# Layer 2's scan: six odd states with a drive scaled by ScalarE and turned by TensorE, y and raw steps in two bank pairs by turns

## The chip, the cores and the metric

The kernel runs on one core of one Trainium2 chip. The metric is the device time of the whole program in microseconds. Engines are named as in the profile: PE is TensorE, PEld its weight loads, DVE is VectorE, ACT is ScalarE, POOL is GpSimd, SP is SyncE. All data here is float32.

## The reference, cut to what matters

x has 16 samples of 64 x 64 places and 128 channels. Four layers are added to it one after the other: linear attention, a Fourier mixing, a selective scan in four directions (layer 2, the one that is changed), and a gated scan in one direction. Layer 2 in short:

```python
xs = stack([x0, x1, x0[..., ::-1], x1[..., ::-1]], axis=1)   # 4 directions, 256 channels, 4096 places
x_dbl = einsum('bkdl,kcd->bkcl', xs, x_proj_w)
dts_r, Bs, Cs = x_dbl[:, :, :R], x_dbl[:, :, R:R + N], x_dbl[:, :, R + N:]   # R = 8, N = 16
dt = softplus(einsum('bkrl,kdr->bkdl', dts_r, dt_proj_w) + dt_proj_b)
def step(h, inp):
    dA = exp(dt_l[..., None] * A)
    h = h * dA + (dt_l * u_l)[..., None] * B_l[:, :, None, :]
    y = einsum('bkdn,bkn->bkd', h, C_l)
    return (h, y)
ys = ys + Ds * xs
```

## The kernel before, in words

A hardware loop runs once per sample; each sample goes through the four layers. The scan of layer 2 (class Scan2, and a function scan2 on each engine) works in **groups**: one group g is one direction k and one chunk c of 512 places, 4 x 8 = 32 groups a sample. Its 256 channels are two halves h of 128 partitions, side by side in 1024 columns. A **unit** u is one of the 16 states n of a group, so there are 512 units a sample. For every unit:

- POOL makes the drive (make_drive, L545): du times the row of B, spread over the partitions by a DMA, into one of six SBUF buffers Q. In front of it stand sum_dt (L528) and make_du (L535) once a group.
- ACT makes the decays (L1026 through act): exp(A dt) of both halves into one of two bank pairs of PSUM, banks 2, 3 or 4, 5 by turns.
- DVE runs two scans (states, L1568). For the states in POOL_STATES the result goes to Q and POOL weighs it with the row of C (weigh, L556); for the others it stays in PSUM and DVE weighs it (weigh, L1576) into Q.
- ACT copies the last column of the state (carry) for the next chunk.
- PE adds Q onto y with an identity matrix (L662), into banks 0 and 1.

Once a group, for the next group, PE multiplies rows of dt, B and C (rows, bank 6), ACT copies them (split), PE makes the raw steps (steps, banks 7 and 6), ACT and DVE work out softplus in two halves: ACT gives abs, exp, relu, the mask, a square and a log (three parts each of two activations, 512 columns), and log_small on DVE (L1533, L1536) puts a series where the log is inexact. DVE takes y out of PSUM in take_y (L1545 in direction 0, L1553 in the others).

The order of the work is written out by hand: every engine has its own list over u, and semaphores tie them. The decays of unit u + 2 wait until unit u has left the same bank pair, a drive waits until the sum of the unit six before has been made, and each engine works its list strictly in order. SP issues the loads of B and C rows, two rows to a DMA, in rings of four buffers each.

Of the kernel before, what the change touches and what calls it, by code (L numbers as in the profile page):

```python
# [20 lines left out]
KDIR = 4  # L21
# [5 lines left out]
POOL_STATES = (1, 4, 6, 9, 12, 14)  # L27
# [40 lines left out]
def program(nc, x_in, consts, d, out):  # L68
# [6 lines left out]
    with ctx:  # L75
# [27 lines left out]
        DTB2 = sb("DTB2", KDIR * 2); AN2 = sb("AN2", KDIR * 2 * SN)  # L103
# [137 lines left out]
        class Scan2:  # L241
# [8 lines left out]
            def __init__(s):  # L250
# [16 lines left out]
                s.b_loaded = [sample_sem(f"s2_b_loaded{i}") for i in range(4)]  # L267
                s.c_loaded = [sample_sem(f"s2_c_loaded{i}") for i in range(4)]
# [12 lines left out]
                s.y_taken = sample_sem("s2_y_taken")  # L281

# [33 lines left out]
            def wide(s, bufs, u):  # L316

                return bufs[u // 2 % 4][:, NT * (u % 2):NT * (u % 2 + 1)]

            def loads(s, u):  # L320

                return 16 * (u // 8 + 1)
# [12 lines left out]
            def like(s, ap, g):  # L335

                if g // NCH % 2 == 0:
# [69 lines left out]
                 (DTW2[32:32 + RANK, :], d["dtw2"]), (DTB2[:, :], d["dtb2"]), (AN2[:, :], d["al2"]),  # L407
# [1377 lines left out]
```

## Time and profile before

| | us |
|---|---|
| median of 3 runs | 40399.08 |
| lowest and highest | 40380.85, 40405.81 |
| profiled execution, its own time | 40396.46 |
| its span, first to last instruction | 40394.6 |
| granted PE clock, mean over the span | 0.875 |

The profile's page gives the busy time of each engine over the span, then 40 slices, the DMA queues, and groups of instructions by line. Nearly every activation has the same line, since a helper records it, so operands and shapes tell them apart. Sixteen samples give sixteen like stretches; layer 2's scan is the largest part of each. PSUM is PS, the six Q, DT, DU and the softplus buffers are all parts of WORK, XN holds rows of B, CWIDE and WORK hold rows of C, and HST the carried states.

### The profile page before, as it was taken

The page shows a single profiled execution, that of the slowest core. Times are in us where ns is not written, and L with a number is a line of the kernel's source. Part 1 is how long each engine was busy: PE and PEld are TensorE (multiplying, and loading weights), DVE is VectorE, ACT ScalarE, POOL GpSimd, SP SyncE. Part 2 cuts the span into 40 slices and gives each one's busy share as a digit, 9 for nine tenths or more (in the row PEclk, how much of TensorE's full clock was granted, in tenths as well). Part 3 has the DMA queues.
Part 4 walks back from the last instruction along what each step waited for, and adds up shares of the span by engine and source line. Part 5 has one row for each costly group of instructions (what it writes and reads, how often), then busy time and mean ns, then how long its engine had stood idle before and what let it go on. Part 6 is the DMA issues. An engine that isn't in the chain of part 4 may idle for free. (4 is left out here: it accounts for less than half of the span.)

```text
span 40394.6 us, 270531 instructions
## 1 busy us (share of the span) xinstructions
PE 29251.1 (72%) x61476; PEld 11541.5 (29%) x61476; DVE 33936.9 (84%) x33869; ACT 19958.1 (49%) x37509; POOL 30996.0 (77%) x14776
## 2 busy tenths in 40 slices
PE   6777777777777777777777777777777777777777
PEld 3232232322323223232232322323223232232322
DVE  7969879698796987969879698796987969879698
ACT  4545545455454554545545455454554545545455
POOL 6949869498694986949869498694986949769497
PEclk8888888888888888888888888888888888888888
DMA  3424324243242432424324243242432424324243
GB/s 104 151 83 152 135 100 151 85 151 134 100 152 84 152 134 101 152 84 152 134 102 151 83 152 134 101 152 84 151 133 103 151 84 151 133 102 152 84 152 132
DMA packets 1387317, 5029.10 MB, mean 124 GB/s; under 512 B 164272, under 2 KB 165816, under 8 KB 1381440
## 3 DMA queue, kind: packets, MB, share of 16 engines
q1 hardware_dynamic: 1385536, 5010.20, 35.5%
q8 instruction: 526, 8.62, 0.1%
q14 instruction: 1255, 10.28, 0.1%
HBM read 4938.25 MB, written 71.30 MB: 124 GB/s over the span
## 5 line engine op out<-in xcount | busy, mean ns | idle before, releaser
L662 PE MATMUL PS<-WORK,CST 128*128 128x512 f32 x36096 | 19792.8, 693 | 8395.9 <-POOL WORK L556 7606.2
L545 POOL TENSOR_TENSOR WORK<-WORK,XN 128x1024 f32<-128x1024 f32 x8192 | 19253.1, 2383 | 1.3
L662 PEld LDWEIGHTS PS<-WORK,CST 128*128 128x128 f32 x36096 | 7532.0, 220 | 20965.6 <-POOL WORK L556 10427.4
L1026 ACT ACTIVATE PS<-WORK,AN 128x512 f32<-128x512 f32 x17408 | 11307.0, 679 | 1984.9 <-DVE WORK L1576 1092.8
L1568 DVE TENSOR_TENSOR_SCAN PS<-PS,HST,WORK 128x512 f32<-128x512 f32 x8960 | 10975.2, 1272 | 45.4 <-ACT PS L1026 32.1
L1568 DVE TENSOR_TENSOR_SCAN WORK<-PS,HST,WORK 128x512 f32<-128x512 f32 x5376 | 6582.9, 1267 | 0.0
L556 POOL TENSOR_TENSOR WORK<-WORK,CWIDE 128x1024 f32<-128x1024 f32 x2048 | 4864.0, 2375 | 118.3 <-issue 65.2
L1026 ACT ACTIVATE HST<-PS 128x2 f32<-128x2 f32 x5152 | 858.6, 167 | 6586.2 <-DVE WORK L1576 6152.6
L632 POOL MEMSET XN<- 128x66 f32 x32 | 4.9, 154 | 5101.7 <-DVE SM L1414 5003.0
L1576 DVE TENSOR_TENSOR WORK<-PS,WORK 128x1024 f32<-128x1024 f32 x3072 | 3763.0, 1225 | 105.2
L1026 ACT ACTIVATE WORK<-PS 40x512 f32<-40x512 f32 (+2 forms) x1600 | 935.5, 598 | 3547.7 <-PE PS L662 2867.3
L1026 ACT ACTIVATE WORK<-PS,DTB 128x512 f32<-128x512 f32 x2304 | 1556.3, 675 | 2144.3 <-DVE WORK L1536 1650.0
L1576 DVE TENSOR_TENSOR WORK<-PS,CWIDE 128x1024 f32<-128x1024 f32 x2048 | 2508.8, 1225 | 70.0
L556 POOL TENSOR_TENSOR WORK<-WORK 128x1024 f32<-128x1024 f32 x1024 | 2438.1, 2381 | 0.0
L528 POOL TENSOR_TENSOR WORK<-WORK 128x512 f32<-128x512 f32 x1024 | 1326.5, 1295 | 1407.2 <-DVE WORK L1536 1407.2
L662 PE MATMUL PS<-XN,TAP 128*128 128x512 f32 x4608 | 2055.2, 602 | 34.6 <-DVE XN L1430 34.6
L662 PE MATMUL PS<-BIG,XP 128*40 128x512 f32 x2304 | 1687.6, 819 | 451.8 <-ACT BIG L1026 294.5
L601 POOL TENSOR_TENSOR WORK<-WORK 128x512 f32<-128x512 f32 x1024 | 1275.1, 1269 | 840.9 <-DMA WORK<-xbc_rows 774.7
L1026 ACT ACTIVATE WORK<-WORK,VEC 128x512 f32<-128x512 f32 x2304 | 1631.4, 708 | 0.0
L1568 DVE TENSOR_TENSOR_SCAN PS<-PS,WORK 128x512 f32<-128x512 f32 x1280 | 1491.0, 1211 | 109.3 <-POOL WORK L545 104.7
L1026 ACT ACTIVATE WORK<-PS,VEC 128x512 f32<-128x512 f32 x896 | 614.1, 685 | 1693.5 <-PE PS L662 1691.1
L535 POOL TENSOR_TENSOR WORK<-WORK,BIG 128x1024 f32<-128x1024 f32 x512 | 1347.8, 2632 | 1.2
(158 smaller groups left out, 25260.5 us busy)
## 6 DMA issues: line engine op xcount, KB each, us to landing
XN<-xbc_rows SPq DMA_DIRECT2D x4096, 512.0 KB, 3.6
WORK<-xbc_rows SPq DMA_DIRECT2D x2816, 512.0 KB, 4.3
CWIDE<-xbc_rows SPq DMA_DIRECT2D x2304, 512.0 KB, 4.2
BIG<-in_spec_dram SPq DMA_DIRECT2D x32, 2048.0 KB, 12.3
X<-in_x_dram SPq DMA_DIRECT2D x68, 512.0 KB, 4.8
xbc_rows<-WORK SPq DMA_DIRECT2D x512, 64.0 KB, 3.1
out_dram<-X SPq DMA_DIRECT2D x64, 512.0 KB, 5.1
xbc_rows<-WORK SPq DMA_DIRECT2D x128, 32.0 KB, 1.6
```

The source lines that it names most:

```text
L528: nc.gpsimd.tensor_tensor(dt, dt, S.LE[:, ch(h)], ADD).then_inc(S.dt_made, 1)
L535: nc.gpsimd.tensor_tensor(S.like(S.DU[g % 2], g), S.like(S.DT[g % 2], g), S.cols(BIG1, g), MUL).then_inc(S.du_ready, 1)
L545: nc.gpsimd.tensor_tensor(S.both(S.Q[u % 6]), S.both(S.DU[u // SN % 2]), S.wide(S.BW, u).unsqueeze(1).to_broadcast([P, 2, NT]), MUL).then_ ...
L556: nc.gpsimd.tensor_tensor(q, q, S.wide(S.CW, u).unsqueeze(1).to_broadcast([P, 2, NT]), MUL).then_inc(S.weighed_pool, 1)
L601: nc.gpsimd.tensor_tensor(S.Q[u % 6], S.DU[u // SN3 % 2], S.wide(S.BW, u), MUL).then_inc(S.drive, 1)
L632: nc.gpsimd.memset(XN3[:, 0, :], 0.0).then_inc(frame_zero, 1)
L662: return nc.tensor.matmul(o, w, r, start=start, stop=stop)
L1026: return nc.scalar.activation(o, i, f, **k)
L1568: r = V.tensor_tensor_scan(o, a, b, HST2[:, 2 * n + h:2 * n + h + 1] if c else 0.0, MUL, ADD)
L1576: V.tensor_tensor(S.both(S.Q[u % 6]), PS[:, lo:lo + 2, :], S.wide(S.CW, u).unsqueeze(1).to_broadcast([P, 2, NT]), MUL).then_inc(S.weighed_ ...
```

## The change

Six odd states (5, 7, 9, 11, 13, 15) get their drive by another road. After du is made, PE turns it (turn_du, at unit 15 of the group before) so that places lie on partitions, and ACT copies it to SBUF as DUT (copy_dut, at unit 1). The row of B is turned too (turn_b at unit 5, copied by copy_bt at unit 6), so that B's value is one number per partition. For a turned unit ACT scales DUT by it, four activations of 256 columns into one buffer ST (scale), and PE turns the eight blocks back into the unit's bank pair (turn_back). The decays of such a unit go to its Q in SBUF, and the scan reads its drive from PSUM. POOL makes no drive for these states, but weighs nine states where it weighed six. DVE weighs seven where it weighed ten.

y and the raw steps share two bank pairs, 0 and 1 or 6 and 7, by turns of the group. The softplus is done once over 1024 columns in six parts, at units 7 to 11, and its bias comes in through a row of ones in the step matmul. The sum on PE comes two units later than its unit, take_y after unit 2 in place of unit 1, the small log once after unit 11 in place of twice after 7 and 10, and sum_dt once at unit 12. The loads of B and C are one row each, in rings of six.

```diff
-POOL_STATES = (1, 4, 6, 9, 12, 14)
+POOL_STATES = (0, 4, 5, 7, 8, 9, 11, 13, 15)
+TURNED_STATES = (5, 7, 9, 11, 13, 15)
...
+                s.CW = [take(NT) for _ in range(4)] + [CWIDE[:, NT * i:NT * (i + 1)] for i in range(2)]
+                s.ST = CWIDE[:, w:2 * w]
+                s.BW = [XN[:, NT * i:NT * (i + 1)] for i in range(6)]
+                s.DUT = XN[:, 6 * NT:6 * NT + w]
...
+            def pair(s, g):
+                return 0 if g % 2 == 0 else 6
...
+            def wait_pair(s, e, u):
+                if s.on_pool(u):
+                    e.wait_ge(s.scanned, u + 1)
+                else:
+                    s.wait_weighed(e, u)
+                    if s.of(u)[1] < NCH - 1:
+                        e.wait_ge(s.carried, s.carried_by(u))
...
+                def turn_b(g):
+                    e.wait_ge(S.rows_copied, g + 1)
+                    for j in range(4):
+                        r = nc.tensor.transpose(bank(S.pair(g) + 1)[:, SN * j:SN * (j + 1)], S.R[0:SN, ch(j, P)], EYE[0:SN, 0:SN])
+                    r.then_inc(S.b_turned, 1)
...
+                    if h == 1:
+                        e.wait_ge(S.bt_copied, g + 1)
...
+                def turn_back(u):
+                    e.wait_ge(S.scaled, 4 * S.turned_by(u))
+                    if u >= 2:
+                        S.wait_pair(e, u - 2)
+                    for h in range(2):
+                        for j in range(4):
+                            r = nc.tensor.transpose(bank(S.banks(u)[h])[:, ch(j, P)], S.ST[:, ch(2 * j + h, P)], EYE)
+                    r.then_inc(S.turned_back, 1)
...
                 for u in range(S.units):
                     g, n = u // SN, u % SN
                     if g + 1 < KDIR * NCH:
+                        if n == 3:
+                            rows(g + 1, 0)
+                            rows(g + 1, 1)
+                        if n == 5:
+                            turn_b(g + 1)
+                        if n == 6:
+                            steps(g + 1, 0)
+                            steps(g + 1, 1)
+                        if n == 15:
+                            turn_du(g + 1)
+                    if u + 2 < S.units and S.is_turned(u + 2):
+                        turn_back(u + 2)
+                    if u >= 2:
+                        sum_up(u - 2)
...
+                def scale(u):
+                    if u % SN == S.turned[0]:
+                        e.wait_ge(S.dut_copied, u // SN + 1)
+                        e.wait_ge(S.bt_copied, u // SN + 1)
+                    if S.turned_by(u) > 1:
+                        e.wait_ge(S.turned_back, S.turned_by(u) - 1)
+                    for j in range(4):
+                        col = SN * j + u % SN
+                        act(S.ST[:, ch(j, 2 * P)], S.DUT[:, ch(j, 2 * P)], ACT.Identity,
+                            scale=S.BT[u // SN % 2][:, col:col + 1]).then_inc(S.scaled, 1)
...
                 for u in range(S.units):
                     g, n = u // SN, u % SN
-                    if u + 1 < S.units:
-                        decays(u + 1)
+                    if u + 3 < S.units and S.is_turned(u + 3):
+                        scale(u + 3)
+                        decays(u + 3)
+                    if n == 1 and g:
+                        copy_dut(g)
                     if g + 1 < KDIR * NCH:
-                        if n == 2:
+                        if n == 5:
                             split(g + 1)
-                        if 4 <= n < 10:
-                            softplus(g + 1, (n - 4) // 3, (n - 4) % 3)
+                        if n == 6:
+                            copy_bt(g + 1)
+                        if n in (7, 8, 9):
+                            softplus(g + 1, n - 7)
+                        if n == 9:
+                            softplus(g + 1, 3)
+                        if n in (10, 11):
+                            softplus(g + 1, n - 6)
                     if S.of(u)[1] < NCH - 1:
                         carry(u)
+                    if u + 2 < S.units and not S.is_turned(u + 2):
+                        decays(u + 2)
...
+                        a, b = (in_sbuf, in_psum) if S.is_turned(u) else (in_psum, in_sbuf)
+                        o = in_sbuf if S.on_pool(u) else in_psum
```

The first place is ACT, the first group of a sample, units 7 to 10 before: the second half's softplus parts among decays (PS<-WORK,AN) and carries (HST).

```order
L1026 ACTIVATE WORK<-PS,DTB 128x512 [waits s2_dt_steps,s2_dt_raw]
L1026 ACTIVATE WORK<-WORK 128x512 [waits s2_softplus]
L1026 ACTIVATE HST<-PS 128x2 [waits s2_weighed_dve]
L1026 ACTIVATE PS<-WORK,AN 128x512 [waits s2_carried,s2_weighed_dve]
L1026 ACTIVATE PS<-WORK,AN 128x512
L1026 ACTIVATE WORK<-PS,DTB 128x512
L1026 ACTIVATE WORK<-WORK,VEC 128x512 [waits s2_softplus]
L1026 ACTIVATE HST<-PS 128x2 [waits s2_weighed_dve]
L1026 ACTIVATE PS<-WORK,AN 128x512 [waits s2_carried,s2_weighed_dve]
L1026 ACTIVATE PS<-WORK,AN 128x512
```

The same engine after, units 8 to 10: CWIDE<-XN,BTR are scalings, WORK<-WORK,AN the decays of a turned unit, 128x1024 the softplus parts.

```order
L1132 ACTIVATE PS<-WORK,AN 128x512 [waits s2_scanned]
L1132 ACTIVATE PS<-WORK,AN 128x512
L1132 ACTIVATE WORK<-PS 128x1024
L1132 ACTIVATE WORK<-WORK,VEC 128x1024 [waits s2_softplus]
L1132 ACTIVATE HST<-WORK 128x2 [waits s2_scanned]
L1132 ACTIVATE CWIDE<-XN,BTR 128x256 [waits s2_turned_back]
L1132 ACTIVATE CWIDE<-XN,BTR 128x256 x3
L1132 ACTIVATE WORK<-WORK,AN 128x512 [waits s2_summed]
L1132 ACTIVATE WORK<-WORK,AN 128x512
L1132 ACTIVATE PS<-WORK,VEC 128x1024 [waits s2_softplus]
L1132 ACTIVATE HST<-PS 128x2 [waits s2_weighed_dve]
L1132 ACTIVATE PS<-WORK,AN 128x512 [waits s2_carried,s2_weighed_dve]
```

Before, one or two activations of 512 columns stand between two pairs of decays. After, four scalings that wait for turned_back, the decays of a turned unit and up to two parts of 1024 columns stand between the decays of one even unit and the next.

The second place is PE. Before, in the second group, units 2 to 4: sums (WORK,CST), and the step matmuls (WORK,DTW), each behind rows_copied.

```order
L662 MATMUL PS<-WORK,CST 128x512 [waits s2_weighed_dve]
L662 MATMUL PS<-WORK,CST 128x512
L662 MATMUL PS<-WORK,DTW 128x512 [waits s2_rows_copied]
L662 MATMUL PS<-WORK,CST 128x512 [waits s2_weighed_dve]
L662 MATMUL PS<-WORK,CST 128x512
L662 MATMUL PS<-WORK,DTW 128x512 [waits s2_rows_copied]
L662 MATMUL PS<-WORK,CST 128x512 [waits s2_weighed_pool]
L662 MATMUL PS<-WORK,CST 128x512
```

After, in the second group, units 4 to 6: turn_b (CST,ROW), turn_back (CST,CWIDE), the steps (ROW,DTW) and the sums.

```order
L722 MATMUL PS<-WORK,CST 128x512 [waits s2_weighed_dve]
L722 MATMUL PS<-WORK,CST 128x512
L892 MATMUL PS<-CST,ROW 128x16 [waits s2_rows_copied]
L892 MATMUL PS<-CST,ROW 128x16 x3
L919 MATMUL PS<-CST,CWIDE 128x128 [waits s2_scanned,s2_scaled]
L919 MATMUL PS<-CST,CWIDE 128x128 x7
L722 MATMUL PS<-WORK,CST 128x512 [waits s2_weighed_dve]
L722 MATMUL PS<-WORK,CST 128x512
L722 MATMUL PS<-ROW,DTW 128x512
L722 MATMUL PS<-ROW,DTW 128x512 [waits s2_bt_copied]
L722 MATMUL PS<-WORK,CST 128x512 [waits s2_weighed_pool]
L722 MATMUL PS<-WORK,CST 128x512
```

The turn back of unit 7 stands behind turn_b, which waits for ACT's copy of the rows, and the one of unit 9 behind the second step matmul, which waits for bt_copied, and behind a sum.

## Rows read from the trace of the kernel before

**Rows 1.** Page, part 1: busy us (share of the span) and instructions of each engine.

```profile
PE 29251.1 (72%) x61476; PEld 11541.5 (29%) x61476; DVE 33936.9 (84%) x33869; ACT 19958.1 (49%) x37509; POOL 30996.0 (77%) x14776
```

**Rows 2.** Windows: one group; stretch, length, PE, PEld, DVE, ACT, POOL busy (count), PEclk, DMA, GB/s.

```profile
494.70:550.20 55.50, 37.21 (x71) 13.82 (x70) 54.15 (x51) 30.71 (x62) 55.50 (x26) 0.88 0.46 154
```

**Rows 3.** Timeline of POOL: start us, us, engine, line, op, out<-in, count [idle before].

```profile
494.70 1.27 POOL L528 TENSOR_TENSOR WORK<-WORK 128x512 f32<-128x512 f32 x1
...
550.20 1.29 POOL L528 TENSOR_TENSOR WORK<-WORK 128x512 f32<-128x512 f32 x1
...
954.17 2.87 POOL L535 TENSOR_TENSOR WORK<-WORK,BIG 128x1024 f32<-128x1024 f32 x1
...
1010.60 2.87 POOL L535 TENSOR_TENSOR WORK<-WORK,BIG 128x1024 f32<-128x1024 f32 x1
```

**Rows 4.** Timeline of DVE, same columns: scans, weighing, take_y, small log.

```profile
512.20 1.23 DVE L1576 TENSOR_TENSOR WORK<-PS,CWIDE 128x1024 f32<-128x1024 f32 x1
513.34 2.45 DVE L1568 TENSOR_TENSOR_SCAN WORK<-PS,HST,WORK 128x512 f32<-128x512 f32 x2
515.71 2.44 DVE L1568 TENSOR_TENSOR_SCAN PS<-PS,HST,WORK 128x512 f32<-128x512 f32 x2
518.18 1.23 DVE L1576 TENSOR_TENSOR WORK<-PS,CWIDE 128x1024 f32<-128x1024 f32 x1
...
526.34 1.41 DVE L1545 SCALAR_TENSOR_TENSOR BIG<-BIG,VEC,PS 128x512 f32<-128x512 f32 x2 [0.93 <-PE PS L662]
...
546.90 0.69 DVE L1533 SCALAR_TENSOR_TENSOR PS<-PS,WORK 128x512 f32<-128x512 f32 x1
547.63 0.73 DVE L1536 COPY_PREDICATED WORK<-WORK,PS 128x512 f32<-128x512 uint32 x1
...
972.35 2.37 DVE L1553 TENSOR_TENSOR BIG<-BIG,PS 128x1024 f32<-128x1024 f32 x1 [0.88 <-PE PS L662]
```

**Rows 5.** Timeline of ACT, same columns: decays, softplus parts, a carry.

```profile
494.48 1.30 ACT L1026 ACTIVATE PS<-WORK,AN 128x512 f32<-128x512 f32 x2
495.71 0.67 ACT L1026 ACTIVATE WORK<-PS,DTB 128x512 f32<-128x512 f32 x1
496.29 0.71 ACT L1026 ACTIVATE WORK<-WORK,VEC 128x512 f32<-128x512 f32 x1
496.90 0.15 ACT L1026 ACTIVATE HST<-PS 128x2 f32<-128x2 f32 x1
497.14 1.30 ACT L1026 ACTIVATE PS<-WORK,AN 128x512 f32<-128x512 f32 x2
```

**Rows 6.** Groups by form, ACT: shapes xcount, busy us, mean ns, idle before.

```profile
L1026 ACT ACTIVATE BIG<-PS 128x512 f32<-128x512 f32 x768 | 433.2, 597 | 490.4 <-PE PS L662 489.8
...
L1026 ACT ACTIVATE BIG<-PS 128x256 f32<-128x256 f32 x64 | 24.6, 384 | 293.4 <-DVE BIG L1488 293.4
...
L1026 ACT ACTIVATE WORK<-WORK 128x1024 f32<-128x1024 f32 x64 | 62.1, 1043 | 0.0
```

**Rows 7.** Timeline of PE: eight transposes; then records of sums in the scan.

```profile
94.20 1.04 PE L725 MATMUL PS<-CST,WORK 128*128 128x128 f32 x8
...
541.09 3.70 PE L662 MATMUL PS<-WORK,CST 128*128 128x512 f32 x8 [1.53 <-POOL WORK L556]
...
548.00 3.78 PE L662 MATMUL PS<-WORK,CST 128*128 128x512 f32 x4 [3.21 <-POOL WORK L556]
```

**Rows 8.** Windows, columns as in Rows 2: transposes alone, and a start after idle.

```profile
94.00:96.00 2.00, 1.66 (x16) 1.42 (x14) 0.36 (x2) 1.09 (x2) 0.00 (x0) 1.00 0.00 0
...
547.00:550.20 3.20, 2.20 (x3) 1.16 (x4) 3.16 (x5) 1.63 (x4) 3.20 (x2) 0.50 0.71 273
```

More of the change, by code:

```diff
@@ L314, in both, with is_turned, turned_by, decay_of @@
                 return ap.rearrange("p (d l) -> p d l", l=NT)
[L316 to L322, printed above, removed]
+            def is_turned(s, u):
+                return u % SN in s.turned
+            def turned_by(s, u):
+                return u // SN * len(s.turned) + sum(n <= u % SN for n in s.turned)
+            def decay_of(s, u):
+                return s.decay_sbuf if s.is_turned(u) else s.decay
+            def decayed_by(s, u):
+                return s.turned_by(u) if s.is_turned(u) else s.driven_by(u)
+            def driven_by(s, u):
+                return u + 1 - s.turned_by(u)
+            def pair(s, g):
+                return 0 if g % 2 == 0 else 6
+            def raw(s, g):
+                return PS[:, s.pair(g):s.pair(g) + 2, :]
+            def loaded(s, i):
+                return 16 * (i // 6 + 1)
+            def wait_pair(s, e, u):
[5 more added lines that the diff above has]
+                        e.wait_ge(s.carried, s.carried_by(u))
             def position(s, g):
@@ L840, in scan2 @@
                     if g + 1 < KDIR * NCH:
-                        if n < 2:
-                            rows(g + 1, n)
-                        if n in (3, 4):
-                            steps(g + 1, n - 3)
-                    S.wait_weighed(e, u)
-                    if n == 0 and g:
-                        e.wait_ge(S.y_taken, g)
-                    for h in range(2):
-                        r = mm(bank(h), EYE, S.Q[u % 6][:, ch(h)], n == 0, n == SN - 1)
-                    r.then_inc(S.summed, 1)
+                        if n == 3:
[12 more added lines that the diff above has]
+                        sum_up(u - 2)
+                sum_up(S.units - 2)
+                sum_up(S.units - 1)
             def block2():
@@ L1157, in softplus @@
                     elif part == 1:
+                        e.wait_ge(S.softplus, 6 * g + 1)
+                        act(S.E, S.LE, ACT.Exp, scale=-1.0).then_inc(S.softplus, 1)
+                    elif part == 2:
                         if g >= 2:
-                            e.wait_ge(S.decay, 2 * SN * (g - 1))
+                            last = SN * (g - 1) - 1
+                            e.wait_ge(S.decay, 2 * S.driven_by(last))
+                            e.wait_ge(S.decay_sbuf, 2 * S.turned_by(last))
@@ L1557, in states @@
                     k, c, n = S.of(u)
-                    e.wait_ge(S.drive, u + 1)
+                    if S.is_turned(u):
+                        e.wait_ge(S.turned_back, S.turned_by(u))
+                    else:
+                        e.wait_ge(S.drive, S.driven_by(u))
                     if c:
```

243 lines of the change are left out of this document (139 added, 104 removed).

## Prediction

> **What bounds the kernel now.** The page first [rows 1]: VectorE 84% and GpSimd 77% of the span, ScalarE 49%, and the same pattern sixteen times. These shares are averages over four layers. The change touches layer 2's scan alone, so I read one chunk group there (16 units, one chunk of one direction). In the window of one group of direction 0 [rows 2] GpSimd is busy 55.50 of 55.50 us and VectorE 54.15. The timeline of GpSimd [rows 3] gives the period: 494.70 to 550.20 is 55.50 us in direction 0, 954.17 to 1010.60 is 56.43 us in direction 1, where the multiply that makes du reads columns turned (2.87 us). Directions 2 and 3 I take as 0 and 1. GpSimd bounds the stage with VectorE 1.3 us behind. In those 55.50 us stand 16 drives, 6 weighings, one du, each 1024 columns, and two 512-column sums (1.27 us): 23 large operations (the count of 26 takes one in at the edge) at (55.50 - 2 x 1.23) / 23 = 2.31 us.
>
> **Removed from GpSimd.** After: 10 drives, 9 weighings, one sum of 1024 and one du, 21 x 2.31 = 48.5 us (49.1 in odd directions). Seven microseconds go from the engine that bounds.
>
> **VectorE.** Start to start [rows 4]: two scans of a unit that GpSimd weighs take 2.37 us (513.34 to 515.71), the others 2.47 (515.71 to 518.18) and their weighing 1.14 (512.20 to 513.34), 3.61 together. Before 10 x 3.61 + 6 x 2.37 = 50.3; after 7 x 3.61 + 9 x 2.37 = 46.6. The two small-log passes of 0.69 + 0.73 become one of 1024 columns; a VectorE operation of 1024 columns in PSUM takes 1.23 [rows 4], so I take 2.45. take_y stays: 1.4 us (direction 0) or 2.37 (direction 1). No scan has had its decay in SBUF and drive in PSUM; both operand places occur singly, and I price it the same, with +0.06 per scan (1 us a group) as the bad end. VectorE's own work is then 50.4 or 51.4 us. If nothing else were late, that would be the period.
>
> **What is late next is ScalarE.** Two decays of 512 cost 1.23 us (494.48 to 495.71), one activation of 512 0.58 to 0.61, a carry from PSUM with the next decay behind it 0.24 [rows 5]. A column costs (0.597 - 0.384) / 256 = 0.83 ns and 1024 columns 1.04 us in all [rows 6]. So a scaling of 256 columns starts 0.61 - 0.21 = 0.40 after the one before: 1.6 us for the four of a turned unit, 9.6 a group; a softplus part of 1024 takes 1.03, six of them 6.2 instead of 12 x 0.6. ScalarE's sum, near 40 us, fits in 50. Its order does not. I lay the instructions out by these durations, with t = 0 where VectorE starts unit 3 of a group and everything earlier ready.
>
> Eight transposes took 1.04 us [rows 7]; four matmul records of a sum at full clock (x8 in 3.70) 1.7 us. 3.7: unit 3 weighed. Only then ScalarE carries it (the carry stands ahead of the scaling for unit 7), and only then can TensorE turn unit 5 back, into unit 3's banks: 5.0. ScalarE scales 7, makes decays 7, carries 4, makes decays 6: 9.4 (0.25 of it waiting for a sum). split, carry 5: 10.05. TensorE has turn_b **ahead** of turn_back(7), and turn_b waits for split: unit 7 is back at 11.6, and the scaling for 9 waits for that. Scale 9, decays 9, the copy of b, carry 6, decays 8: 16.3. Softplus part 0, carry 7: 17.4. turn_back(9) stands behind the second step matmul, which waits for the copy of b (14.85), and behind sum_up(4): 14.85 + 0.86 + 1.7 + 1.04 = 18.5. Then scale 11, decays 11, part 1, carry, decays 10: 23.8. Parts 2 and 3: 25.9. Scale 13, decays 13, part 4, carry, decays 12: 31.3. Part 5: 32.4. From 3.7 that is 28.7 us, 24.4 of work and 4.3 of waits on TensorE's queue.
>
> VectorE without waits reaches the small log after units 3 to 11, (3, 6 and 10 of 3.61, six of 2.37): 25.0. By the steps above it waits 0.55 before unit 6, 0.9 before 8, 0.35 before 9, 2.4 before 10 and 3.15 before the small log, 7.4 in all. The small log needs part 5, so it ends at 34.85. Units 12 to 15 and 0 to 2 follow at VectorE's pace (4 x 3.61 + 3 x 2.37 = 21.55; ScalarE's four jobs per pair of units are 4.3 us with no softplus among them), take_y 1.35 or 2.3: 57.7 us in direction 0, 58.7 in 1. Waits queued elsewhere are covered: GpSimd's sum of dt waits for the small log, then needs 3 x 2.31 us to the first drive of the next group while VectorE has 12 us of units 12 to 15. SyncE issues 26 loads of one row for 16 of two, less traffic than the 154 GB/s of [rows 2], into rings of six, with weighings six units back to wait for.
>
> **Sum.** +2.2 and +2.3 us a group against 55.50 and 56.43. Of 32 groups a sample the last has no softplus of a next one and gains VectorE's 50.3 - 46.6 = 3.7, say 4 us. 16 x (31 x 2.25 - 4) = 1,050 us. The pieces ahead of the first group and the constants are costed at nothing: the turn of du there hides behind the first drive. The profiled execution took 40,396 us, 3 us under the median shown, so **41,450**.
>
> **Rivals.**
>
> *The chain without its waits.* TensorE's queue costs less than I laid out and only the 24.4 us of work and one turn (1.3) stay. Then part 5 ends at 29.3, and the period is 54.6 or 55.6: -0.85 a group, 39,910 us. For it: each wait is under 2 us and depends on how exactly the engines meet. Against it: the order of TensorE's queue is fixed and turn_b truly waits for split.
>
> *VectorE bounds (faster).* If ScalarE runs ahead more than I allow, so that part 5 is there when unit 11 ends, the period is VectorE's 50.4 or 51.4: -5.1 x 31 - 4 a sample, 37,800 us. It decides when ScalarE needs under 21.3 us for what I count as 24.4 + 1.3. For it: both old bounds shrink for certain. Against it: 17% fewer microseconds than the rows give.
>
> *A slow TensorE (slower still).* The granted clock fell in this stage: after an idle of 1.53 us the eight records took 3.70, after 3.21 us four took 3.78 [rows 7] at a granted 0.50, the 1.2 GHz level [rows 8]. In the new order TensorE sits idle about 7 us before unit 15 is turned, and about 2.8 us twice before unit 5. If units 5 to 11 meet the low clock, the three turns on the chain double (+0.87 each), the step matmul too (+0.86) and sum_up(4) (+1.7): +5.2 a group, 44,000 us. Against it: from 3.7 to 30 TensorE has work two thirds of the time. A stretch of nothing but transposes ran at a granted 1.00 [rows 8], though behind other matmuls. The Trainium skill, TensorE: Matmul & The Clock Gate, Part 4, says that transposes do not count as TensorE activity as matmuls do; by it the 64 new ones would help less to hold the clock, which leans to this rival; the stretch just named neither bears it out nor refutes it.
>
> *No difference.* The layout's gain and the chain's loss cancel within 0.2%, some 80 us, about what a measurement of this kernel can tell from no change.
>
> **Chances.** Forecast 0.53; slow TensorE 0.12; chain without waits 0.16 (0.11 faster, 0.03 same, 0.02 slower); VectorE bounds 0.16; cancelling 0.03. So faster 0.27, same 0.06, slower 0.67. The range takes the forecast, the chain without waits (39,910) and half of the slow TensorE (+2.6 a group, 42,700): 39,850 to 42,700 leaves out VectorE's bound and full slowness, 2 in 10.
>
> **What would show it.** In the profile after: a period near 58 us from du to du; GpSimd no longer full (some 49 busy); ScalarE without gaps over 1.6 us from unit 4 to the small log; VectorE waiting for ScalarE before units 8 and 10 and some 3 us before the small log. Wrong if VectorE has no wait over 1 us before the small log (second rival), if the scalings start over 0.45 or under 0.35 us apart, if eight transposes take about 1.9 us between units 5 and 11 (slow TensorE), or if the waits stand before other units than 6 to 11.

## The result, and the profile after

| | before | after |
|---|---|---|
| median, us | 40402.26 | 42912.14 |
| lowest and highest | 40380.85, 40405.81 | 42883.87, 42947.69 |
| ratio, 95% interval | | 1.0623, 1.0604 to 1.0641 |
| span of the profiled execution | 40394.6 | 42881.9 |

The change makes the kernel 6.2% slower, 2,510 us. The forecast was slower, and 41,450 us; the time lies 212 us above the range. First the page of after, part 1, beside [rows 1], then part 4, the chain that ended last:

```profile
PE 31957.7 (75%) x92196; PEld 14932.2 (35%) x92196; DVE 32162.6 (75%) x30798; ACT 24681.1 (58%) x47749; POOL 27597.9 (64%) x12728
...
PE 34%; ACT 26%; DVE 16%; POOL 11%; issue 10%; DMA 2%; SPq 1%; POOLq 0%; ACTq 0%; DVEq 0%
```

GpSimd and VectorE both lost work, as the change meant, and neither is near full. PE and ACT carry 60% of the chain, which is that of the whole program: the time goes back and forth between the two engines that got the new road of the drive.

Windows of after, columns as in [rows 2]: one group of direction 0 and one of direction 1, each from one multiply that makes du to the next; then three stretches within the first group.

```profile
703.91:765.29 61.38, 45.43 (x132) 21.57 (x132) 50.61 (x45) 39.85 (x81) 48.88 (x21) 0.89 0.35 113
947.44:1009.02 61.58, 45.86 (x132) 20.66 (x132) 51.24 (x44) 39.77 (x81) 49.50 (x22) 0.89 0.35 113
...
735.00:739.50 4.50, 4.01 (x15) 1.85 (x14) 4.42 (x4) 3.50 (x9) 4.50 (x3) 1.00 0.49 131
739.90:746.50 6.60, 6.60 (x14) 3.45 (x14) 2.92 (x3) 2.19 (x6) 2.04 (x1) 0.50 0.38 122
747.00:752.00 5.00, 5.00 (x19) 2.54 (x17) 2.29 (x3) 4.63 (x9) 3.51 (x2) 1.00 0.33 80
```

The period is 61.4 us where 57.7 was forecast; GpSimd is busy 48.9 (48.5 forecast), VectorE 50.6 (50.4), ScalarE 39.9 ("near 40"). So the work of these three engines was priced rightly and the waits were not. The granted clock is 1.00, then 0.50, the 1.2 GHz level, then 1.00 again, in the middle of a stretch in which TensorE is busy.

Timeline of PE in that group, columns as in [rows 3], L919 turn_back, L892 turn_b, the L722 records with ROW the step matmuls, those with WORK,CST the sums:

```profile
728.38 1.09 PE L919 MATMUL PS<-CST,CWIDE 128*128 128x128 f32 x8
729.31 3.60 PE L722 MATMUL PS<-WORK,CST 128*128 128x512 f32 x8
734.42 0.41 PE L892 MATMUL PS<-CST,ROW 16*128 16x16 f32 x4 [1.51 <-ACT ROW L1132]
734.76 1.09 PE L919 MATMUL PS<-CST,CWIDE 128*128 128x128 f32 x8
735.69 1.88 PE L722 MATMUL PS<-WORK,CST 128*128 128x512 f32 x4
737.51 1.12 PE L722 MATMUL PS<-ROW,DTW 9*128 9x512 f32 x2
739.11 1.47 PE L722 MATMUL PS<-ROW,DTW 9*128 9x512 f32 x2 [0.48 <-ACT BTR L1132]
740.51 3.78 PE L722 MATMUL PS<-WORK,CST 128*128 128x512 f32 x4
744.08 1.92 PE L919 MATMUL PS<-CST,CWIDE 128*128 128x128 f32 x8
```

Turning 5 and 7 back runs at full speed (1.09 us). Then the second step matmul takes 1.47, the sum of unit 4 3.78 where its neighbour took 1.88, and turn_back(9) 1.92. ScalarE, same view, at the scalings (CWIDE<-XN,BTR, four records each) of units 7, 9 and 11, and then VectorE at its waits:

```profile
729.51 1.70 ACT L1132 ACTIVATE CWIDE<-XN,BTR 128x256 f32<-128x256 f32 x4 [1.41 <-PE PS L919]
...
735.89 1.71 ACT L1132 ACTIVATE CWIDE<-XN,BTR 128x256 f32<-128x256 f32 x4 [1.44 <-PE PS L919]
...
746.04 1.71 ACT L1132 ACTIVATE CWIDE<-XN,BTR 128x256 f32<-128x256 f32 x4 [4.30 <-PE PS L919]
```

```profile
733.37 2.47 DVE L1717 TENSOR_TENSOR_SCAN PS<-PS,HST,WORK 128x512 f32<-128x512 f32 x2 [0.76 <-ACT PS L1132]
...
740.03 2.46 DVE L1717 TENSOR_TENSOR_SCAN WORK<-PS,HST,WORK 128x512 f32<-128x512 f32 x2 [0.58 <-ACT PS L1132]
746.04 2.45 DVE L1717 TENSOR_TENSOR_SCAN WORK<-WORK,HST,PS 128x512 f32<-128x512 f32 x2 [3.54 <-PE PS L919]
751.20 2.47 DVE L1717 TENSOR_TENSOR_SCAN PS<-PS,HST,WORK 128x512 f32<-128x512 f32 x2 [2.71 <-ACT PS L1132]
...
760.17 1.23 DVE L1678 SCALAR_TENSOR_TENSOR PS<-PS,WORK 128x1024 f32<-128x1024 f32 x1 [2.89 <-ACT WORK L1132]
```

Unit 3 starts on VectorE at 724.18, so these are 5.3, 11.7 and 21.9 us in the forecast's count, which had 5.0, 11.6 and 18.5. Up to turn_back(7) the layout is right within 0.3 us; turn_back(9) is 3.4 late, and everything behind it with it.

### The profile page after: what moved, and what is told of

The parts are those of the page before. It is cut to its first block, busy times and chain, and to the rows that moved or that the text cites. A ratio compares the mean times of both kernels' runs of the same rounds, so it can differ in the third digit from the quotient of the medians.

```text
span 42881.9 us, 337204 instructions
## 1 busy us (share of the span) xinstructions
PE 31957.7 (75%) x92196; PEld 14932.2 (35%) x92196; DVE 32162.6 (75%) x30798; ACT 24681.1 (58%) x47749; POOL 27597.9 (64%) x12728
## 4 chain that ended last, share of the span: by engine, by line
PE 34%; ACT 26%; DVE 16%; POOL 11%; issue 10%; DMA 2%; SPq 1%; POOLq 0%; ACTq 0%; DVEq 0%
PE PS L722 27%; ACT WORK L1132 11%; ACT CWIDE L1132 7%; POOL WORK L608 7%; PE PS L919 6%; ACT PS L1132 6%; POOL WORK L619 4%; DVE PS L1717 4%; DVE WORK L1717 3%; DVE PS L1678 1%; DMA CWIDE<-xbc_rows 1%; DVE PS L1810 1%; ACT BIG L1132 1%; ACT ROW L1132 1%; PE PS L892 0%
## 5 line engine op out<-in xcount | busy, mean ns | idle before, releaser
L722 PE MATMUL PS<-WORK,CST 128*128 128x512 f32 x36096 | 18666.1, 654 | 2490.9 <-POOL WORK L619 2419.0
L608 POOL TENSOR_TENSOR WORK<-WORK,XN 128x1024 f32<-128x1024 f32 x5120 | 12037.9, 2357 | 3001.6 <-PE PS L722 2959.6
L722 PEld LDWEIGHTS PS<-WORK,CST 128*128 128x128 f32 x36096 | 7004.1, 208 | 11025.0 <-issue 8681.9
L1717 DVE TENSOR_TENSOR_SCAN PS<-PS,HST,WORK 128x512 f32<-128x512 f32 x6272 | 7700.3, 1274 | 1680.5 <-ACT PS L1132 1680.5
L619 POOL TENSOR_TENSOR WORK<-WORK 128x1024 f32<-128x1024 f32 x3072 | 7240.8, 2357 | 1916.7 <-DVE WORK L1717 1432.8
L1132 ACT ACTIVATE PS<-WORK,AN 128x512 f32<-128x512 f32 x11264 | 7326.0, 679 | 1018.5 <-DVE WORK L1725 464.5
L919 PE MATMUL PS<-CST,CWIDE 128*128 128x128 f32 x24576 | 3957.9, 314 | 4652.9 <-DVE WORK L1717 4608.0
L1717 DVE TENSOR_TENSOR_SCAN WORK<-WORK,HST,PS 128x512 f32<-128x512 f32 x5376 | 6569.3, 1264 | 1135.7 <-PE PS L919 1135.6
L1132 ACT ACTIVATE CWIDE<-XN,BTR 128x256 f32<-128x256 f32 x12288 | 5217.1, 495 | 3820.1 <-PE PS L919 3819.3
L919 PEld LDWEIGHTS PS<-CST,CWIDE 128*128 128x128 f32 x24576 | 3312.2, 163 | 6925.5 <-issue 6911.9
L1132 ACT ACTIVATE WORK<-WORK,AN 128x512 f32<-128x512 f32 x6144 | 4078.9, 711 | 143.8 <-PE PS L722 125.0
L1717 DVE TENSOR_TENSOR_SCAN WORK<-PS,HST,WORK 128x512 f32<-128x512 f32 x2688 | 3287.4, 1265 | 242.3 <-ACT PS L1132 242.3
L590 POOL TENSOR_TENSOR WORK<-WORK 128x1024 f32<-128x1024 f32 x512 | 1198.3, 2340 | 1504.6 <-DVE WORK L1681 1449.0
L722 PE MATMUL PS<-XN,TAP 128*128 128x512 f32 x4608 | 2051.1, 601 | 34.6 <-DVE XN L1575 34.6
L722 PE MATMUL PS<-BIG,XP 128*40 128x512 f32 x2304 | 1690.5, 862 | 297.0 <-ACT BIG L1132 297.0
```

What stands on the lines that cost most here:

```text
L590: nc.gpsimd.tensor_tensor(dt, dt, S.LE, ADD).then_inc(S.dt_made, 1)
L608: nc.gpsimd.tensor_tensor(S.both(S.Q[u % 6]), S.both(S.DU[u // SN % 2]), S.BW[i % 6].unsqueeze(1).to_broadcast([P, 2, NT]), MUL).then_inc( ...
L619: nc.gpsimd.tensor_tensor(q, q, S.CW[u % 6].unsqueeze(1).to_broadcast([P, 2, NT]), MUL).then_inc(S.weighed_pool, 1)
L722: return nc.tensor.matmul(o, w, r, start=start, stop=stop)
L919: r = nc.tensor.transpose(bank(S.banks(u)[h])[:, ch(j, P)], S.ST[:, ch(2 * j + h, P)], EYE)
L1132: return nc.scalar.activation(o, i, f, **k)
```

## The experiments

All ran against the kernel before, 3 rounds each. "Mean period" is the mean over the four directions, from the first and last start of the multiply that makes du in the first sample, 29 periods apart: (2294.5 - 520.3) / 29 = 61.18 by this row of after (view of one source line; duration min/median/max, first and last start); for the kernel before they are 508.7 and 2131.6.

```profile
L598 POOL TENSOR_TENSOR WORK<-WORK,BIG x30: 2342/2850/2860, 520.3 to 2294.5; 128x1024 f32<-128x1024 f32 x30
```

| kernel | us | ratio [95%] | mean period |
|---|---|---|---|
| before | 40402 | 1 | 55.96 |
| after | 42912 | 1.0623 [1.0604, 1.0641] | 61.18 |
| e1_fill_matmul | 42920 | 1.0622 [1.0604, 1.0640] | 61.18 |
| e1_fill_transpose | 42911 | 1.0622 [1.0604, 1.0640] | 61.18 |
| e2_turnb_late | 42094 | 1.0419 [1.0402, 1.0436] | 59.49 |
| e3_sum4_late | 42888 | 1.0613 [1.0595, 1.0631] | 60.89 |
| e4_parts_spread | 43914 | 1.0861 [1.0834, 1.0888] | 63.17 |
| e5_combo | 43208 | 1.0699 [1.0683, 1.0714] | 61.70 |
| e6_no_turned | 40478 | 1.0025 [1.0010, 1.0039] | 56.30 |
| e7_fill_all | 42127 | 1.0431 [1.0413, 1.0448] | 59.44 |
| e8_two_turned | 40163 | 0.9941 [0.9925, 0.9958] | 55.51 |
| e9_three_turned | 39917 | 0.9882 [0.9866, 0.9899] | 55.14 |
| e10_four_turned | 40854 | 1.0112 [1.0095, 1.0129] | 57.09 |
| e11_fill_early | 42126 | 1.0435 [1.0417, 1.0452] | 59.70 |
| e12_fill_late | 41612 | 1.0310 [1.0293, 1.0327] | 58.51 |
| e13_three_early_log | 39744 | 0.9846 [0.9830, 0.9863] | 54.74 |
| e14_fill_15 | 41936 | 1.0382 [1.0365, 1.0399] | 59.07 |
| e15_fill_0 | 42277 | 1.0466 [1.0449, 1.0484] | 59.92 |

### The change without its turned states

```diff
-POOL_STATES = (0, 4, 5, 7, 8, 9, 11, 13, 15)
-TURNED_STATES = (5, 7, 9, 11, 13, 15)
+POOL_STATES = (1, 4, 6, 9, 12, 14)
+TURNED_STATES = ()
```

> The changed kernel with no turned state and the old six states weighed by GpSimd; the one softplus of 1024 columns, the two bank pairs, the loads of one row, and the turn of b and du with their copies stay. If the loss stands in the turned drives (the chain), GpSimd bounds again at 55.5 us plus 0 to 2 for its wait on the later small log: 40,400 to 41,400 us. If it stands in the rest of the change, it stays near 42,900.

40,478 us. The bank pairs, the whole softplus, the later sums, the one-row loads and the turns of du and b, which stay, cost 76 us together in this kernel. GpSimd bounds it again (55.42 of 55.50 us busy), so what they cost the other engines can be hidden behind GpSimd here. The six turned drives, with the weighings that moved to GpSimd, cost the other 2,434.

### Is it the gap ahead of turn_b?

```diff
                         if n == 5:
+                            free = bank(S.pair(g + 1) + 1)
+                            mm(free, EYE, CST[:, 0:NT])
+                            mm(free[:, 0:256], EYE, CST[:, 0:256])
                             turn_b(g + 1)
```

> The changed kernel, with one matmul of 512 and one of 256 columns put on TensorE ahead of turn_b, into the free bank of the pair, where TensorE sits idle 1.5 us for ScalarE's split. Nothing reads them; the results stay. Theory A (the slow TensorE between units 6 and 9 is the step that I mis-sized, and it comes from too little matmul work ahead of it): the sum of unit 4 takes 1.9 us in place of 3.8 and turn_back(9) 1.04 in place of 1.92, 3.4 us a group less, 41,200 us. Theory B (the low clock has nothing to do with that gap): 42,900 us, within 100.

The same with twelve transposes in that place:

> The same place filled with twelve transposes of 128x128 in place of the matmuls, 1.3 us of TensorE as well. If transposes keep the clock as matmuls do, the time is that of the run with matmuls, 41,200 us under theory A. If they do not, the low stretch stays: 42,900 us, within 100, while the run with matmuls is faster. Under theory B both are at 42,900.

42,920 and 42,911 us: no change, and the low clock stands where it stood. e1_fill_matmul, timeline of PE:

```profile
742.45 3.78 PE L722 MATMUL PS<-WORK,CST 128*128 128x512 f32 x4
746.03 1.92 PE L919 MATMUL PS<-CST,CWIDE 128*128 128x128 f32 x8
```

The gap right ahead of the low clock is not its cause. My first theory fell.

### turn_b out of the way of turn_back(7)

```diff
-                        if n == 5:
-                            turn_b(g + 1)
...
                         turn_back(u + 2)
+                    if n == 5 and g + 1 < KDIR * NCH:
+                        turn_b(g + 1)
```

> The changed kernel with turn_b behind turn_back(7) in TensorE's order. By the chain (ScalarE waits for turn_back(7), which waits behind turn_b for split) the scaling for unit 9 starts 1.45 us earlier and all up to the small log with it: 1.45 x 496 groups = 720 us less, 42,190 us. The rival, that only the low clock at the sum of unit 4 sets the chain, gives no change: 42,900. If the clock falls elsewhere or not at all as well, up to 3.4 us a group more comes off, 40,500.

42,094 us, 100 below the expectation and 818 below after. Timeline of PE, e2_turnb_late:

```profile
717.14 3.07 PE L722 MATMUL PS<-WORK,CST 128*128 128x512 f32 x4 [2.73 <-POOL WORK L619]
...
728.55 0.42 PE L892 MATMUL PS<-CST,ROW 16*128 16x16 f32 x4 [0.64 <-ACT ROW L1132]
...
735.28 1.04 PE L919 MATMUL PS<-CST,CWIDE 128*128 128x128 f32 x8
```

turn_b stands behind turn_back(7) now, and turn_back(9) takes 1.04 us in this group: the low clock has moved to the sum of unit 0, at 717.14. In five of the seven groups of direction 1 it still meets turn_back(9) (1.76 to 1.92 us). So order and clock are mixed in this gain.

### The sum of unit 4 out of the way of turn_back(9)

```diff
-                    if u >= 2:
+                    if u >= 2 and n != 6:
+                        if n == 7:
+                            sum_up(u - 3)
                         sum_up(u - 2)
```

> The changed kernel with the sum of unit 4 behind turn_back(9), ahead of the sum of unit 5. If the late turn_back(9) alone is what ScalarE waits for, it is back 3.6 us earlier and the time is 1,800 us less, 41,100. By the chain as the trace shows it, the decays of unit 11 wait for the sum of unit 5 in the same Q buffer, and that sum comes no earlier, so VectorE starts unit 9 sooner and waits before unit 10 instead: 42,900 us, within 150.

42,888 us. Timelines of e3_sum4_late, ScalarE at the decays of unit 11, then VectorE at unit 10:

```profile
750.39 1.33 ACT L1134 ACTIVATE WORK<-WORK,AN 128x512 f32<-128x512 f32 x2 [3.04 <-PE PS L722]
...
753.47 2.47 DVE L1719 TENSOR_TENSOR_SCAN PS<-PS,HST,WORK 128x512 f32<-128x512 f32 x2 [4.66 <-ACT PS L1134]
```

The chain's account held: VectorE no longer waits before unit 9, but the later sums hold up the decays of 11 by 3.04 us, and VectorE waits 4.66 before unit 10. Here a slow piece of TensorE's queue was not passed by reordering, since both sides of it feed the same ScalarE list.

### The softplus parts spread over units 7 to 12

```diff
-                        if n in (7, 8, 9):
+                        if 7 <= n < 13:
                             softplus(g + 1, n - 7)
-                        if n == 9:
-                            softplus(g + 1, 3)
-                        if n in (10, 11):
-                            softplus(g + 1, n - 6)
```

with the small log after unit 12 and sum_dt at 13.

> The changed kernel with one softplus part a unit at units 7 to 12 (before: 7, 8, two at 9, 10, 11), the small log after unit 12 and the sum of dt on GpSimd at unit 13. If ScalarE's work up to the small log is the chain, VectorE gets unit 12 done while part 5 is made; I count 0.8 us a group less, 400 us, 42,500. If the low clock alone is the loss, no change: 42,900.

43,914 us, a miss of 1,414 in the wrong direction. Timelines of e4_parts_spread, DVE, then POOL:

```profile
726.65 2.46 DVE L1713 TENSOR_TENSOR_SCAN PS<-PS,HST,WORK 128x512 f32<-128x512 f32 x2 [1.29 <-POOL WORK L608]
...
775.32 1.23 DVE L1674 SCALAR_TENSOR_TENSOR PS<-PS,WORK 128x1024 f32<-128x1024 f32 x1 [2.78 <-ACT WORK L1132]
```

```profile
777.95 2.34 POOL L590 TENSOR_TENSOR WORK<-WORK 128x1024 f32<-128x1024 f32 x1 [4.47 <-DVE WORK L1677]
```

The wait before the small log stays at 2.78, and GpSimd, which has to make dt, du and drives from it, now stands 4.47 us for the log (in the group of after shown it does not) and hands the next group's drive of unit 1 over 1.29 late. The prediction's "covered" sum of dt was covered by one unit only. That is part of the loss: VectorE also waits 0.94 before unit 5 and 1.41 before unit 6 (0 and 0.76 in after), behind a sum of unit 0 that takes 3.54 us where after has 1.96, while its wait before unit 9 falls to 2.22. The late turn_b, the late sum and this spread together (e5_combo):

> All three orders together: turn_b behind turn_back(7), the sum of unit 4 behind turn_back(9), one softplus part a unit. If their gains add as by the chain: 1.45 + 0 + 0.8 us a group, 1,120 us less, 41,800. If the low clock goes too, 40,100 to 41,000, level with the kernel before at best.

43,208 us, also a miss: VectorE waits 4.8 us for the decays of 10, as in e3_sum4_late, and keeps the 1.3 for the drive.

### The clock: filling TensorE's idle places

In after, TensorE stands idle for 7 us ahead of turn_back(15), and 1.2 and 2.7 us ahead of the sums of units 15 and 0 (the text for e14_fill_15 below calls them 0 and 1):

```profile
707.52 1.94 PE L919 MATMUL PS<-CST,CWIDE 128*128 128x128 f32 x8 [6.99 <-DVE WORK L1717]
...
719.93 1.98 PE L722 MATMUL PS<-WORK,CST 128*128 128x512 f32 x4 [1.18 <-POOL WORK L619]
724.66 1.96 PE L722 MATMUL PS<-WORK,CST 128*128 128x512 f32 x4 [2.74 <-POOL WORK L619]
```

```diff
+                    if g + 1 < KDIR * NCH and n == 13:
+                        e.wait_ge(S.dt_steps, 2 * g + 4)
+                        for _ in range(6):
+                            mm(bank(S.pair(g + 1)), EYE, CST[:, 0:NT])
                     if u + 2 < S.units and S.is_turned(u + 2):
...
                         e.wait_ge(S.dut_copied, g + 1)
+                        for _ in range(3):
+                            mm(bank(S.pair(g)), EYE, CST[:, 0:NT])
```

e7_fill_all has both and the filling ahead of turn_b; e11_fill_early both; e14_fill_15 the first alone; e15_fill_0 the second alone.

> The changed kernel with matmuls that nothing reads in three idle places of TensorE: six of 512 columns ahead of turn_back(15) (7 us idle there), three ahead of the sum of unit 0 (2.7 us) and 1.5 ahead of turn_b (1.5 us). If the low clock at the sum of unit 4 comes from idle time anywhere ahead of it, it goes: 3.4 us a group less, 41,200 us. If it comes from something else, the sum of unit 4 still takes 3.8 us and the time stays at 42,900 us, within 200.

> This is the kernel of the change with six unneeded matmuls of 512 columns ahead of turn_back(15) and three ahead of the sum of unit 0, and nothing ahead of turn_b. With all three places filled the clock stayed at 1.00 through a group of direction 0 (period 57.88 us against 61.4); with only the gap before turn_b filled nothing changed. Theory A, the low clock at the sum of unit 4 comes of TensorE's two long idle stretches earlier in the group: the clock stays at 1.00 in direction 0 as before, period near 57.9, 42,130 us within 100. Theory B, it takes all places together: the eight transposes of turn_back(9) still take 1.9 us in direction 0, the period stays near 61.4 and the time near 42,900 us.

> Only the six unneeded matmuls ahead of turn_back(15), in the idle stretch of 7 us; nothing ahead of the sum of unit 0 or turn_b. Theory C, the long stretch is what brings the later low clock: the clock stays at 1.00 at the sum of unit 4 in direction 0, the period is near 57.9 us there and the time near 42,130 us, as with both places filled. Theory D, the two waits of 1.2 and 2.7 us around the sums of units 0 and 1 bring it: the eight transposes of turn_back(15) take 1.04 us, those of turn_back(9) still 1.92 us, and the time stays near 42,900 us.

> Only the three unneeded matmuls ahead of the sum of unit 0; the idle stretch of 7 us ahead of turn_back(15) stays. Theory D: the clock stays at 1.00 at the sum of unit 4 in direction 0 although turn_back(15) still takes 1.9 us, and the time falls towards 42,130 us. Theory C: the sum of unit 4 still takes 3.8 us and the time stays near 42,900 us. If both this run and e14_fill_15 reach 42,130 us, either place alone is enough; if neither does, both are needed.

Both early places together: 42,126 us, the same with or without the one ahead of turn_b. Windows of e11_fill_early, two stretches of direction 0, each as long as a group, and a stretch of direction 1, then its PE:

```profile
694.96:752.85 57.89, 47.75 (x151) 21.93 (x150) 50.62 (x45) 39.76 (x81) 48.90 (x22) 1.00 0.36 119
752.85:810.70 57.85, 47.72 (x151) 21.92 (x150) 50.57 (x45) 39.79 (x81) 48.84 (x22) 1.00 0.36 120
935.00:992.00 57.00, 49.52 (x139) 21.80 (x138) 48.64 (x42) 39.21 (x80) 46.95 (x21) 0.94 0.36 118
```

```profile
731.85 1.99 PE L722 MATMUL PS<-WORK,CST 128*128 128x512 f32 x4
733.68 1.04 PE L919 MATMUL PS<-CST,CWIDE 128*128 128x128 f32 x8
```

At a granted 1.00 throughout, the period is 57.9 us: the layout's 57.7. The same place, in the fourth of the groups below, in e14_fill_15 (first alone) and e15_fill_0 (second alone):

```profile
729.92 3.45 PE L722 MATMUL PS<-WORK,CST 128*128 128x512 f32 x4
733.21 1.04 PE L919 MATMUL PS<-CST,CWIDE 128*128 128x128 f32 x8
```

```profile
728.55 3.78 PE L722 MATMUL PS<-WORK,CST 128*128 128x512 f32 x4
732.12 1.91 PE L919 MATMUL PS<-CST,CWIDE 128*128 128x128 f32 x8
```

In these two groups each place by itself leaves the slow sum of unit 4, and the first shortens the low stretch enough to spare turn_back(9). But it depends on the group. The periods of direction 0 in the first sample, between the starts of the multiply that makes du, in us:

| kernel | | | | | | |
|---|---|---|---|---|---|---|
| after | 61.03 | 61.23 | 61.37 | 61.38 | 61.41 | 59.26 |
| e7_fill_all | 57.88 | 61.20 | 59.54 | 57.89 | 57.88 | 57.18 |
| e11_fill_early | 59.54 | 57.89 | 57.88 | 57.88 | 57.87 | 57.21 |
| e14_fill_15 | 57.89 | 57.88 | 61.20 | 59.54 | 57.89 | 57.23 |
| e15_fill_0 | 57.89 | 57.88 | 61.21 | 61.33 | 59.69 | 60.05 |

The sum of unit 4 in the second of these groups, in e14_fill_15 and then in e15_fill_0:

```profile
610.65 1.99 PE L722 MATMUL PS<-WORK,CST 128*128 128x512 f32 x4
```

```profile
609.04 1.98 PE L722 MATMUL PS<-WORK,CST 128*128 128x512 f32 x4
```

So the same order of work meets the low clock in one group and not in the next. Each place alone spares some groups, both together spare four or five of these six, and neither theory holds as a rule. By time e14_fill_15 is the best of these (41,936). Its fifth group ran at a granted 1.00 in 57.89 us, as with both places filled, so in direction 0 the second filling costs nothing; the gain stands in direction 1, where the seven periods run from 58.30 to 60.59 us, against 59.63 to 61.30 with both. In a group of direction 2 of e11_fill_early VectorE still waits 3.6 us for turn_back(9).

> The unneeded matmuls ahead of turn_back(15) and of the sum of unit 0, and turn_b moved behind turn_back(7). At full clock the move takes the wait for split (1.5 us) out of the way of turn_back(7), so that the scaling of 9 and all behind it comes 1.5 us sooner: a period near 56.4 in direction 0. Over the run with all places filled (42,127 us) that is 1.5 x 31 x 16 = 740 us, so 41,400 us, if the clock behaves as it did there. Rival: the order of the matmuls decides which of them meet the low clock, the odd directions keep theirs, and the time stays within 41,800 to 42,100 us, where each part alone is.

41,612 us: 515 of the 740 expected, so order and clock add in the main, but the clock did not stay as it was. Timeline of PE, e12_fill_late, the sum of unit 4:

```profile
732.23 3.58 PE L722 MATMUL PS<-WORK,CST 128*128 128x512 f32 x4
```

### Fewer turned states

The tables alone change: e8_two_turned has TURNED_STATES (13, 15) and POOL_STATES (1, 3, 5, 8, 10, 13, 15); e9_three_turned turns 5 as well; e10_four_turned turns (5, 11, 13, 15) and weighs (0, 3, 5, 8, 9, 11, 13, 15) on GpSimd.

> The changed kernel with two turned states (13, 15) and GpSimd weighing 1, 3, 5, 8, 10, 13, 15. By the chain theory the turning is dear only where ScalarE makes the softplus (units 5 to 11): GpSimd then has 23 large operations, 53.1 us (53.7 in odd directions), VectorE 52.9 or 53.9; period near 53.7, 2.3 us under the kernel before, 39,300 us. If each turned state costs what the six cost over none (2,430 / 6 = 405 us), it is 41,290.

> Three turned states (5, 13, 15), GpSimd weighing 1, 3, 5, 8, 10, 13, 15: GpSimd 22 large operations, 50.8 us, VectorE 52.9 or 53.9 and now the bound, plus half a microsecond of waits: 39,350 us by the chain theory. 41,690 if each turned state costs 405 us.

> Four turned states (5, 11, 13, 15), GpSimd weighing 0, 3, 5, 8, 9, 11, 13, 15: GpSimd 50.8 us, VectorE 51.6 or 52.6 alone, but one scaling stands among the softplus parts, and I expect 1 to 2 us of waits for ScalarE before unit 10 and the small log: 53.6 a group, 39,200 us, level with three. 42,100 if each turned state costs 405 us.

40,163, 39,917 and 40,854 us. Two and three turned states beat both kernels (the one before by 0.6 and 1.2%), though by far less than I had expected; four don't. The rival of 405 us for each turned state (41,290, 41,690 and 42,100) is out. In e9_three_turned one wait is left on VectorE, before the small log (waits of DVE over two groups: total, times, longest):

```profile
DVE PS L1678 <- ACT WORK L1132: 3.8, 2, 1.9
```

In e8_two_turned VectorE waits up to 0.85 for GpSimd's drive as well. In e10_four_turned the wait before the small log is 2.9 us, with 1.5 more before unit 10 (one group of direction 0). The scaling for 11 stands there in front of the softplus parts, behind which that for 13 stands already; that this is the reason was not tried apart from the GpSimd table, which changed too. The last run took the wait of e9_three_turned away by making part 5 right behind part 4:

```diff
-                        if n in (10, 11):
-                            softplus(g + 1, n - 6)
+                        if n == 10:
+                            softplus(g + 1, 4)
+                            softplus(g + 1, 5)
```

> This is the kernel with three turned states (5, 13, 15; 39,917 us) with softplus part 5 moved from unit 11 to unit 10, right behind part 4. There VectorE's only wait is 1.90 us before the small log, for part 5, which ended at 721.99 while part 4 ended at 719.59. Theory: part 5 then ends near 720.6 and 1.4 us of the 1.90 go, the carry and the decays of unit 12 come 1.1 us later but are not needed before the small log ends: period 53.5 in direction 0, 39,917 - 1.4 x 31 x 16 = 39,220 us. Rival: GpSimd (21 large operations of 2.31 us and the weighings it waits for) or the later decays take the wait over, and the time stays near 39,900 us.

39,744 us, the fastest of all, 1.5% under the kernel before. A quarter of the expected gain came. Timeline of DVE, e13_three_early_log:

```profile
717.32 1.23 DVE L1679 SCALAR_TENSOR_TENSOR PS<-PS,WORK 128x1024 f32<-128x1024 f32 x1 [0.59 <-ACT WORK L1132]
...
726.49 2.47 DVE L1718 TENSOR_TENSOR_SCAN PS<-PS,HST,WORK 128x512 f32<-128x512 f32 x2 [0.57 <-ACT PS L1132]
```

The wait went from 1.90 to 0.59 as laid out, and 0.57 came back before unit 14, whose decays stand on ScalarE behind the scaling of 15. Waits of VectorE over the 29 periods of the first sample (total, times, longest), e9_three_turned, then e13_three_early_log:

```profile
DVE PS L1678 <- ACT WORK L1132: 54.7, 29, 2.1
```

```profile
DVE PS L1679 <- ACT WORK L1132: 16.8, 29, 0.8
DVE BIG L1699 <- PE PS L722: 11.9, 14, 1.4
DVE PS L1718 <- ACT PS L1132: 8.0, 16, 0.8
```

Of the 37.9 us gained before the small log 21.7 came back as waits for decays (8.0) and for TensorE's sums before take_y (11.9, and 1.8 in direction 0); the 29 periods are 11.8 shorter. The rival of the expectation, that the later decays take the wait over, is thus right in part; the wait before take_y stood in no expectation.

## Why the prediction was right and wrong

**Right.** GpSimd's 7 us were gained and bought no time; VectorE's own work and the new scans (decay in SBUF, drive in PSUM) came as priced, 1264 ns in the groups of after by form, against 1274 for the others, without the +0.06; the scalings start 0.40 us apart (four in 1.70), the 1024-column parts take 1.00 to 1.14. ScalarE's ordered list with its round trips to TensorE sets the group, and the waits stand before the units named: 0.76 before 6 (0.55 forecast), 0.58 before 8 (0.9), 2.71 before 10 (2.4), 2.89 before the small log (3.15).

```profile
L1717 DVE TENSOR_TENSOR_SCAN PS<-PS,HST,WORK 128x512 f32<-128x512 f32 x6272 | 7700.3, 1274 | 1680.5 <-ACT PS L1132 1680.5
L1717 DVE TENSOR_TENSOR_SCAN WORK<-WORK,HST,PS 128x512 f32<-128x512 f32 x5376 | 6569.3, 1264 | 1135.7 <-PE PS L919 1135.6
```

The second row is the turned units' scans, and their idle is the term that failed. Of the parts costed at nothing e6_no_turned found 76 us, 0.15 us a group (its mean period in the first sample is 0.34 longer).

**Wrong** was one term: "turn_back(9) stands behind the second step matmul ... and behind sum_up(4): 14.85 + 0.86 + 1.7 + 1.04 = 18.5". It came to 21.9, because the last part of these three ran at the granted 0.50: the second step matmul cost 0.35 more (1.47 for 1.12, where the layout had 0.86), the sum 1.9 (3.78 for 1.88, where it had 1.7), the turn 0.88 (1.92 for 1.04). VectorE's wait before unit 9 is 3.54 instead of 0.35, and ScalarE stands 4.30 us before the scaling for 11, where no gap over 1.6 was forecast. All waits are 10.5 us against 7.4; the other 0.6 of the 3.7 us missed is VectorE's own work and the seams between its pieces, 61.4 - 10.5 = 50.9 where the layout had 50.3. Over all directions the mean period is 61.18 against a forecast 58.2: 2.98 x 31 x 16 = 1,480 us, and the time was missed by 1,462. In the group of direction 1 shown above (61.58 against 58.7) the sum of unit 4 takes 3.64 but turn_back(9) 1.04, and VectorE waits 2.22 before unit 9.

**The rival was on the list, and mispriced in chance.** "A slow TensorE" named this mechanism, its place, and the sign by which to know it (eight transposes in about 1.9 us between units 5 and 11). It got 0.12, against it standing that "TensorE has work two thirds of the time". That was no reason: the 6.60 us of the low window were busy from end to end, and the 13 us ahead of them held no idle stretch over 1.51. The idle places that the rival named (7 us ahead of turn_back(15), about 2.8 us twice before unit 5) came as 6.99, 1.18 and 2.74. The prediction read [rows 7] two ways: it took the 3.70 us of eight records for a sum at full clock, and again for a sign that the clock had fallen. The first is right: in that kernel the clock was granted 1.00 from 541 to 545 us, and in after eight records take 3.60 at full clock. Only the second row, 3.78 for four, was at 0.50. And the new transposes are 60 a group (48, 8 and 4), not 64. Its price of +5.2 was too high, since turn_back(5), turn_back(7) and most of the step matmul were spared: 44,000 is 1,090 us too slow, 41,450 is 1,460 too fast. The range took in half of it; 2.98 of 5.2, nearly six tenths, came.

**Cause and what is open.** Shown: the clock term exists and is worth 3.5 us a group in direction 0 (61.4 to 57.9). One kernel shows it by itself: e15_fill_0 takes 57.88 and then 61.21 us for two groups in a row with the same work in the same order, the sum of unit 4 1.98 and then 3.78. And the term goes in four or five of six groups of direction 0 (e7_fill_all, e11_fill_early) when TensorE's two early idle places are filled, though the filling ends 33 and 17 us before the sum of unit 4 (698.75 and 714.4 against 731.85 in e11_fill_early). The Trainium skill, TensorE: Matmul & The Clock Gate, HAM oscillation, ties a loss of the clock to the wait directly ahead of it; at 707.52 the trace agrees (1.94 us for eight transposes behind 6.99 idle), at 739.9 it does not. The same page, Part 4, says that transposes do not count as activity as matmuls do. e1 put matmuls and transposes into the same place and neither did anything, so no run here tells that. Open: why the clock falls in a busy stretch at all, why it does so in one group and not in the next, and why directions 1, 2 and 3 keep low stretches with both early places filled.

## What to carry to other kernels

When work moves from a full engine to two half-full ones, lay out the order of their queues, not their sums: here six round trips between ScalarE and TensorE in a 16-unit group cost more than the 7 us that GpSimd gave up, while three gave a gain. Where TensorE is part of such a chain, price each of its steps at both clock levels and give the slow one a real chance, busy or not, and read several groups before you say where it falls. A step that looks covered (sum_dt, one unit later) should be checked for how much it is covered by: here, in e4_parts_spread, the cover was one unit.

## What the runs showed of the hardware

The granted clock fell to 0.50 for 6.6 us (739.9 to 746.5 in after) although TensorE had been busy, but for 1.51 and 0.48 us, since 726.54. The same place of the same code met the low clock in one group and not in the group before it (e15_fill_0: 3.78 and 1.98 us for the sum of unit 4). Unneeded matmuls that ended 33 and 17 us ahead of that place went with a granted 1.00 in five of six groups of direction 0 (e11_fill_early); with turn_b moved as well the sum of unit 4 took 3.58 (e12_fill_late); with one place alone some groups were spared and some not (e14_fill_15, e15_fill_0). Unneeded matmuls made a kernel faster by 976 us (e14_fill_15 against after), 2.3%.
